# Moving a row projection into the program before it, and an adjacency copied to half precision in memory

## The reference

```python
x = x + gat(layernorm(x), adj)            # softmax over scored edges, then att @ (h @ fc_w + fc_b)
x = x + capacity_ffn(layernorm(x))        # router over 64 experts decides how much of y a row keeps
                                          # y = gelu(h @ w1.T + b1) @ w2.T + b2, same weights for all
# mean aggregation
h = layernorm(x)
deg = sum(adj, axis=1) + 1e-5
out = (adj / deg @ h) @ W_neigh.T + b_neigh + h @ W_self.T + b_self
x = x + relu(out)
x = x + expert_ffn(layernorm(x))          # 8 experts, two a row: (silu(a) * g) @ W2
```

## Time and profile before

| | us |
|---|---|
| median of 3 runs | 1261.61 (1255.98 to 1263.65) |
| profiled execution | 1258.48 |
| its span, first to last instruction | 1256.6 |
| PE, DVE, ACT, POOL busy | 1058.0, 848.2, 691.8, 121.2 |
| mean granted clock of PE | 0.931 |

### The profile page before, as it was taken

One profiled execution on the slowest core, in us unless ns is written; L12 is line 12 of the kernel. 1 busy time (PEld: TensorE's weight loads), 2 busy tenths in 40 slices (PEclk: granted clock), 3 DMA queues, 4 the chain that ended last, 5 costly groups with the idle time before them and its releaser, 6 DMA issues. The chain is left out here.

```text
span 1256.6 us, 24125 instructions
## 1 busy us (share of the span) xinstructions
PE 1058.0 (84%) x7768; PEld 857.3 (68%) x7769; DVE 848.2 (67%) x1916; ACT 691.8 (55%) x752; POOL 121.2 (10%) x122
## 2 busy tenths in 40 slices
PE   4759999999999799898789999981199999999930
PEld 3548888888888688787568888871056666666620
DVE  7469999999994656766734676675255565565526
ACT  2669999999982777774455555530033333333310
POOL 1000000000000000000000132224011211211210
PEclk9889999999999699999889999995599999999975
DMA  9937777777700212110357678721621111111127
GB/s 286 286 113 229 218 246 216 234 224 220 242 18 1 77 68 101 68 35 1 126 210 290 263 285 309 296 89 64 261 111 54 50 54 54 50 54 54 47 85 261
DMA packets 71546, 186.91 MB, mean 149 GB/s; under 512 B 7777, under 2 KB 57824, under 8 KB 62144
## 3 DMA queue, kind: packets, MB, share of 16 engines
q1 hardware_dynamic: 51152, 138.38, 33.5%
q10 hardware_dynamic: 11616, 29.76, 6.5%
q0 software_dynamic: 8720, 17.99, 4.9%
HBM read 140.75 MB, written 45.35 MB: 148 GB/s over the span
## 5 line engine op out<-in xcount | busy, mean ns | idle before, releaser
L586 PE MATMUL PS<-G,PT 128*128 128x256 f16 x2028 | 230.3, 273 | 0.0
L586 PEld LDWEIGHTS PS<-G,PT 128*128 128x128 f16 x2028 | 198.8, 98 | 22.8
L1343 PE MATMUL sum<-H,adjTh 128*128 128x257 f16 x676 | 154.4, 276 | 7.7 <-ACT adjTh L1290 7.7
L1345 PE MATMUL sum<-H,adjTh 128*128 128x256 f16 x676 | 154.4, 275 | 0.0
L1748 DVE SCALAR_TENSOR_TENSOR hb<-ePsH,w_unscale,eb 128x1024 f32<-128x1024 f32 x59 | 75.7, 1284 | 86.4 <-PE ePsH L1669 86.4
L1669 PE MATMUL ePsH<-W,xT_hi 128*128 x472 | 122.5, 382 | 4.7 <-DVE xT_lo L1739 4.7
L1705 ACT ACTIVATE xT_hi<-ePsX 128x256 f16<-128x256 f32 x59 | 22.6, 384 | 177.6 <-PE ePsX L1658 177.6
L1689 PE MATMUL ePsY<-W,actT 128*128 x472 | 111.6, 380 | 0.2 <-issue 0.2
L573 PE MATMUL PS<-ident,probs 128*128 128x128 f32 x676 | 90.0, 280 | 22.2 <-DVE PT L434 20.5
L434 DVE SCALAR_TENSOR_TENSOR PT<-PS,PT 128x1024 f16<-128x1024 f32 x104 | 103.4, 1016 | 4.4 <-ACT PT L283 4.4
L573 PEld LDWEIGHTS PS<-ident,probs 128*128 128x128 f32 x676 | 76.3, 144 | 31.9 <-issue 23.9
(11 more groups left out here) (271 smaller groups left out, 1931.2 us busy)
## 6 DMA issues: line engine op xcount, KB each, us to landing
adjf<-adj_dram SPq DMA_DIRECT2D x26, 1664.0 KB, 8.2
adjTf<-adjT_dram SPq DMA_DIRECT2D x26, 1664.0 KB, 8.7
slot_rows<-blank SPq DMA_DIRECT2D x26, 1028.0 KB, 11.2
c_w<-eW_dram ACTq DMA_DIRECT2D x8, 1024.0 KB, 5.0
xs<-slot_rows SPq DMA_DIRECT2D x59, 128.5 KB, 2.0
d_stage<-eW_dram ACTq DMA_DIRECT2D x7, 1024.0 KB, 8.0
results<-results_dram ACTq DMA_DIRECT2D x12, 512.0 KB, 9.4
eb<-eb_dram SPq DMA_DIRECT2D x1, 4096.0 KB, 13.9
```

Source lines behind the costliest of these rows:

```text
L586: mm = nc.tensor.matmul(acc[u][:, 0:D], left, right, start=(j == 0 and n == 0), stop=(j == T - 1 and n == 2))
L1343: nc.tensor.matmul(acc[u][:, 0:D + 1], left, H[:, j, 0:D + 1], start=(j == 0), stop=False, skip_group_check=True)
L1345: mm = nc.tensor.matmul(acc[u][:, 0:D], left, H[:, j, D + 2:2 * D + 2], start=False, stop=(j == T - 1), skip_group_check=True)
```

## The change

Five things change.

1. `normalised_projection` is gone. `capacity_ffn` projects the rows itself: from chunk 8 on each chunk finishes two pairs of row tiles (`row_group(c)`, r0 and r1), takes mean and variance by `bn_aggr`, and normalises them (`normalise_rows`). In the next chunk PE turns them (`turn_rows`) behind hidden parts 0 and 1, and projects them (`project_rows`) behind hidden parts 2 and 3, with W_self and W_neigh side by side (512 columns) in two fp16 parts. ACT and DVE make the fp16 parts of the turned rows (`rows_hi`, `rows_lo`) and take the result out of psR, one PSUM bank for each of the two rows of a pair: the W_neigh half as high and low part into H (`neighbour_hi`, `own_and_lo`), the W_self half with the bias into `own`. Pairs 8 to 12 are projected after the last chunk. The square root of the variances is on ACT (`row_deviation`) once a chunk.
2. `mean_aggregation` therefore adds projected rows: no turning of the mean, no second projection. One operation takes the sum, scales it by the degree and adds `own`. Rows of a pair are turned and routed one loop turn later than their sum, not two, and the row buffers hold four pairs.
3. The adjacency is copied to fp16 in memory by DMAs on POOL's queue (`adjT16`), 12 tiles during `attention` and 14 during `capacity_ffn` with three in flight. The aggregation loads fp16 tiles into four buffers, when it begins, and casts nothing.
4. The scales of the experts' first weights come from their largest absolute value by row (`expert_peak`, a reduction on DVE in chunks 2 to 9) and are one for all experts; the second weights are loaded and squared too.
5. G is one buffer, not two, and many arrays of `capacity_ffn` lie where later programs keep W1, H and `own`.

```diff
@@ attention, gpsimd
+            for i in range(CAST_EARLY):
+                pool.wait_ge(mask_ready, 2 * i + 2)
+                pool.dma_start(dram["adjT16"][i, :, :], dram["adjT"][i, :, :]).then_inc(cast_done, 16)
@@ capacity_ffn
+        NPAIRS, ROWS_AT = T // 2, 8
+        def row_group(c):
+            first = 2 * (c - ROWS_AT)
+            return range(max(first, 0), min(first + 2, NPAIRS))
@@ gpsimd
+            for i in range(CAST_EARLY, T):
+                n = i - CAST_EARLY
+                wait(pool, cast_done[n % 3], 16 * (n // 3))
+                pool.dma_start(dram["adjT16"][i, :, :], dram["adjT"][i, :, :]).then_inc(cast_done[n % 3], 16)
@@ tensor
+            def project_rows(r):
+                pe.wait_ge(rowT_lo, r + 1)
+                for s in range(2):
+                    wait(pe, own_ready, 2 * (r - 1) + s + 1)
+                    for n, (left, right) in enumerate(((0, 0), (0, 1), (1, 0))):
+                        for k in range(KD):
+                            mm = nc.tensor.matmul(psR[s][:, :], rowT[r % 2][left][:, k, s * P:(s + 1) * P],
+                                                  wsn_p[right][:, k, :], start=(n == 0 and k == 0),
+                                                  stop=(n == 2 and k == KD - 1))
+                    mm.then_inc(proj_done, 1)
+            for c in range(NCH + 3):
                 for b in range(4):
...
                        hidden_part(c, b)
...
+                    for r in row_group(c - 1)[b % 2:b % 2 + 1]:
+                        if b < 2:
+                            turn_rows(r)
+                        else:
+                            project_rows(r)
...
                        output_part(c - 1, b)
@@ scalar, in chunk c
                 gelu(c, 0)
                 gelu(c, 1)
                 gelu_hi(c, 0)
-                if 2 <= c < 2 + E1:
-                    expert_square(c - 2)
+                if c == 10:
+                    second_square(0)
+                if c == 11:
+                    second_square(1)
+                for r in row_group(c - 1)[0:1]:
+                    rows_hi(r)
+                for r in row_group(c - 2)[1:2]:
+                    neighbour_hi(r)
                 gelu(c, 2)
                 gelu_hi(c, 1)
                 gelu(c, 3)
                 gelu_hi(c, 2)
+                for r in row_group(c - 1)[1:2]:
+                    rows_hi(r)
                 gelu_hi(c, 3)
+                for r in row_group(c - 1)[0:1]:
+                    neighbour_hi(r)
+                row_deviation(c)
@@ vector, in chunk c
                 gelu_lo(c, 0)
                 gelu_lo(c, 1)
-                if c >= 8:
-                    residual(4 * c - 32, 4 * c - 30)
+                if 2 <= c < 2 + E1:
+                    expert_peak(c - 2)
+                for r in row_group(c - 2)[1:2]:
+                    own_and_lo(r)
+                for r in row_group(c - 1)[0:1]:
+                    rows_lo(r)
+                for r in row_group(c)[0:1]:
+                    residual(r)
                 gelu_lo(c, 2)
+                for r in row_group(c - 1)[1:2]:
+                    rows_lo(r)
+                for r in row_group(c)[1:2]:
+                    residual(r)
                 gelu_lo(c, 3)
+                for r in row_group(c - 1)[0:1]:
+                    own_and_lo(r)
+                invert_deviation(c)
+                for r in row_group(c):
+                    normalise_rows(r)
@@ after the chunks, vector
+            take(NCH - 2); own_and_lo(7); rows_lo(8); rows_lo(9); residual(10); residual(11); own_and_lo(8)
+            invert_deviation(NCH); normalise_rows(10); normalise_rows(11)
+            take(NCH - 1); residual(12); own_and_lo(9); rows_lo(10); rows_lo(11); invert_deviation(NCH + 1)
+            normalise_rows(12); own_and_lo(10); expert_sums(); own_and_lo(11); rows_lo(12); expert_scales(); own_and_lo(12)
@@ mean_aggregation
+            for i in range(NADJ):
+                sp.dma_start(adjh[i][:, :], adjv[i, :, :]).then_inc(adj_in[i], 16)
-                nc.scalar.copy(adjh[u][:, :], adjf[u][:, :]).then_inc(half_ready, 1)
-                    turn_mean(i - 1, 1)
-                    project(i - 2, 0)
+                v.scalar_tensor_tensor(own[:, i, :], acc[u][:, 0:D], rdegree[u][:, :], own[:, i, :], ALU.mult,
+                                       ALU.add).then_inc(out_ready, 1)
```

More of the change, by code:

```diff
@@ new lines, in rows_hi, with neighbour_hi @@
+            def rows_hi(r):
+                act.wait_ge(rows_turned, r + 1)
+                wait(act, proj_done, 2 * (r - 1))
+                nc.scalar.activation(rowT[r % 2][0][:, :, :], psT[r % 2][:, :].rearrange("p (k n) -> p k n", k=KD),
+                                     ACT.Copy, scale=H_SCALE).then_inc(rowT_hi, 1)
+            def neighbour_hi(r):
+                for s in range(2):
+                    act.wait_ge(proj_done, 2 * r + s + 1)
+                    nc.scalar.activation(H[:, 2 * r + s, 0:D], psR[s][:, D:2 * D], ACT.Copy,
+                                         scale=1.0 / (ROW_BOUND * H_SCALE)).then_inc(HN_hi, 1)
@@ L1332, in _, with deviation, second_copy @@
-            act.wait_ge(ones_set, 1)
-            for i in range(0, TOTAL, 2):
-                body(i)
+            def deviation(i):
+                act.wait_ge(moments_ready, i + 2)
+                wait(act, rstd_ready, i // 2)
+                nc.scalar.activation(std[:, :], moments[(i // 2) % 2][:, :, 1], ACT.Sqrt, bias=eps[:, :]).then_inc(std_ready, 1)
+            def second_copy(i):
+                act.wait_ge(h_ready, i + 2)
+                for u in range(2):
+                    nc.scalar.copy(rows[:, row_slot(i), u, 1, 0:D], rows[:, row_slot(i), u, 0, 0:D]).then_inc(copy_ready, 1)
@@ L1336, in _, with products @@
         @block.tensor
         def _(pe):
-            def products(t, u):
-                pe.wait_ge(half_ready, t + 1)
-                wait(pe, agg_ready, t - 1)
-                for j in range(T):
-                    left = adjh[u][:, j * P:(j + 1) * P]
+            def products(i, first, last):
+                u = i % 2
+                if first == 0:
+                    pe.wait_ge(adj_in[i % NADJ], 16 * (i // NADJ) + 16)
+                    wait(pe, out_ready, i - 1)
+                for j in range(first, last):
+                    left = adjh[i % NADJ][:, j * P:(j + 1) * P]
@@ L1569, in expert_ffn @@
+            for q in range(NROW):
+                pool.wait_ge(scattered[q], 64 * ((T // 2 + NROW - 1 - q) // NROW))
 def expert_ffn(nc, t, dram):
```

773 lines of the change are left out of this document (403 added, 370 removed).

## The result

The changed kernel takes 1362.56 us (median of 4 runs, 1358.95 to 1365.91) against 1259.94 for the kernel before (median of 4). The ratio is 1.0815, 95% interval 1.0768 to 1.0861: slower, as forecast, but by 103 us and not by 40, and outside the range of 1248 to 1350.

A forecast was written before the change was run, and what follows sets the result against it. PE was taken as the limit in long stretches, with chains of small steps at the seams. 1258.5 - 40 (aggregation) - 40 (projection program) + 121 (feed-forward program) = 1299.5, plus 3.1 to the median: 1302 us, range 1248 to 1350.

The forecast's parts named there:

- the start of the feed-forward program: Two more weight loads and a Square, beside three copies, delay the feed-forward program's start: +8 us, ends 2 to 20.
- The slow copies: Rival: copies through POOL's queue end some 105 us after the feed-forward program is done; 1405 us, chance 0.08.
- The two waits a chunk: Chunks 9 to 12: PE idles before projecting each pair's rows, 4.8 us for the first pair, 6.5 for the second.
- Added work and clock: Feed-forward program: 3.0 us more PE work a pair; PE's clock after gaps costs 15 us, ends 0 and 45.
- The squares in chunks 10 and 11: A Square of 1.9 us on ACT stands ahead of the copy of r0's rows in these chunks: +4 us.
- The maxima: Expert maxima in the feed-forward program become eight DVE reductions of 2.3 us each: +7 us, 0 to 12.
- the other five: Of the eight DVE reductions for the expert maxima, five lie in idle DVE time.
- The end of the program: After the feed-forward program's last chunk, five pairs are still projected one behind the other: 31.7 us against 13.4, +18.
- The walk: Following three queues through the feed-forward program's end: projection of pair 9 starts at 8.5 us, the end comes at 31.7.
- The aggregation: No turning or projecting of the mean, -28 us; first tile's load, +2; shorter end, -14; in all -40.
- Covered waits: Rival: DVE and ACT run far enough ahead that projections in the feed-forward program never wait; 1245 us, chance 0.13.
- The range: Whole kernel: 1248 to 1350 us, with 0.2 chance outside; the forecast's lenient end was given as 1266.

The follow-up runs named there:

- e1_paced: The changed kernel, but POOL asks for one adjacency copy a chunk of the feed-forward program, not three at once from its start: 1306.72 us, ratio 1.0383 to the kernel before.
- e2_pieces: The changed kernel, but each adjacency tile copied in the feed-forward program is asked for as four pieces of 832 columns: 1316.94 us, ratio 1.0464 to the kernel before.
- e3_cover: The changed kernel with its row work reordered on PE, ACT and DVE, pairs projected one chunk later behind hidden parts 0 and 1: 1296.23 us, ratio 1.0300.
- e4_squares: The changed kernel, but the bound on the experts' first weights is their sum of squares on ACT, not largest values on DVE: 1354.29 us, ratio 1.0767.
- e7_copy_only: The kernel before, plus only the adjacency's fp16 copy during attention and fp16 loads into four buffers, without ACT's casts: 1251.67 us, ratio 0.9931.
- e5_all: The changed kernel with the edits of e1_paced, e3_cover and e4_squares together: 1233.03 us, ratio 0.9791 to the kernel before.
- e6_early: As e5_all, but all 26 adjacency copies are asked for during attention and none in the feed-forward program: 1230.30 us, ratio 0.9759 to the kernel before.

## Why the prediction was wrong

- **The step that failed** is "a third stream is not shown; I take **+8**, near the row of two streams, and 2 to 20 as ends", the start of the feed-forward program. It measured +57.3. The prices of 5.0 and 8.0 came from loads of the experts' weights, which have 7.3 KB a packet (1023 packets for 7.45 MB between 450 and 540 in the kernel before). The question that was not asked is how large a packet of each stream is: a copy of a contiguous tile moves 18 KB a packet, the load of the second weights 1 KB, and for each of its packets it lets one of the copies pass. The experts' loads show the other case: beside a copy they took 7.8 us (e1_paced) and not 4.8. e1_paced and e2_pieces show the cause from two sides. The 14 copies take 14 x 4.1 = 57 us, and the second weights landed 64.7 us after their issue against 8.5 before, 56 later. With the measured +57 in place of +8 the sum is 1302 + 49 = 1351.
- **The slow copies**, a rival at 1405, had the wrong end of it. The copies were fast, one every 4.1 us and not every 18 or 30, and the end of the program did not wait for them. What was waited for were the loads beside them.
- **The two waits a chunk** were forecast at 4.8 and 6.5 us and measured 5.5 and 6.2 (21.8 and 24.9 over four chunks), with the releasers that the order had shown. This part of the mechanism was right. e3_cover shows that they come from the order and not from the load of ACT and DVE. Missed was one wait of 6.1 us in chunk 9, for the first normalised rows: later chunks hide it, since PE is late by then anyway.
- **Added work and clock.** Of the +97 in chunks 9 to 12, 52.8 are those waits, and PE's busy time grew from 41.9 to 86.0, by 44.1. At full clock I count 6.0 a chunk, 24, for the new matmuls, so some 20 are the clock, granted at 0.79 there. e3_cover agrees: the 130 matmuls of a chunk took 16.9 us at a clock of 1.00 and 21.9 at 0.80, 5.0 a chunk. The forecast was 15 for the clock, for the end of the program too. The squares in chunks 10 and 11, forecast at 4, seem to have cost 2.8: the first wait is 5.95 and 5.94 there and 4.56 in chunk 12, which has none. That comparison is between chunks and was not tried by itself.
- **The maxima** were forecast at +7 with 12 as the end. The stretch grew by 12.6, of which e4_squares takes back 8.7. The term counted the reductions and not the lower clock that the gaps bring, 5.9 of the 12.6. Nor do the other five all lie in idle time, as the prediction had it: the one of chunk 9, 2.28 us (L1135 at 630.88), stands on DVE directly ahead of the low part of the first rows, within the first wait, 5.39 us there.
- **The end of the program**, +18 forecast, +18.6 measured. The walk held too: counted from its start, the projections of pairs 9 and 10 began at 7.9 and 16.8 us, forecast 8.5 and 17.9.
- **The aggregation** was forecast at -28 + 2 - 14 and measured -29.0 + 1.2 - 15.9. The -29.0 is the right number for a reason that was only partly right: PE's busy time in the loop fell by 24.4 (193.6 to 169.2), and 4.6 more are idle time that was there before; e7_copy_only traces most of that idle time, 3.2 us, to ACT's casts. The row stretches of PE overlap, so 1.08 a tile was somewhat too much for the work.
- **Covered waits**, the rival at 1245, was rightly the less likely for this kernel. e5_all is near what it describes, and gave 1233, but with the copies paced and the maxima gone as well.
- **The range.** Its lower end was added up wrong: 1302 less 15, 6, 7 and 4 is 1270 and not 1266. That changes nothing here.

One question is left open. Whether rows projected inside the feed-forward program are better than a program of their own with both weights was not tried. In e6_early the feed-forward program takes 244.4 us, 15.7 more than the two programs before, and the aggregation saves 43.

## What to carry to other kernels

Before a transfer is called hidden, ask which loads somebody waits for in the same stretch, and compare the packets of the two, not their bytes: a large contiguous copy beside a load in small rows takes nearly all of the bandwidth until it is done. Put such a copy where loads are asked for long enough ahead, or pace it, or cut it into pieces with smaller packets. And a full engine with waits in its queue order is cheap to mend: look at what stands directly ahead of the instruction that the waiting engine needs, on each of the engines, and put work whose inputs are ready ahead of work on the part that was only just begun.

## What the runs showed of the hardware

- Copies within memory with a change from single to half precision ran at 832 KB written in 4.11 us, 207 GB/s, with packets of 18 KB and with pieces whose rows have 1.7 KB alike, where no load was under way beside them; in attention 26 of them cost no measurable time at a DMA share of 0.87, though the loads beside them took 14.5 us and not 8.2.
- Three queues with work pending had 452, 455 and 457 packets in 40 us, of 18, 1.0 and 0.35 KB each; with the copies in pieces of 1.5 KB packets it was 911, 1191 and 1222 in 13 us.
- SP's instruction that asks for a load took 6.03 to 10.29 us (three of them, 414 to 441 in the changed kernel) while the loads on its queue were held up, and the same three 0.4 to 0.6 in e2_pieces: here a queue that is held up also held up the engine that fills it.
